# A branch prefetch hint at the head of the four long edge loops of a graph network on one core

## The reference

```python
def mesh_conv(x, src, dst, ea, w1, b1, g, bt, w2, b2):
    m = jnp.concatenate([x[dst], x[src], ea], axis=-1) @ w1 + b1
    m = jax.nn.silu(group_norm(m, g, bt))
    m = m @ w2 + b2
    out = jax.ops.segment_sum(m, dst, num_segments=n)
    return out / jnp.clip(cnt, 1.0)[:, None]
...
logits = (q[dst] * k[src]).sum(-1) * scale + (edge_attr @ ew + eb)
amax = jax.ops.segment_max(logits, dst, num_segments=n)
pe = jnp.exp(logits - amax[dst])
o = jax.ops.segment_sum(w[:, :, None] * v[src], dst, num_segments=n)
...
return h + o
```

## Time and profile before

| what | us |
|---|---|
| median of 3 runs | 8504.54 |
| lowest and highest | 8486.66, 8512.32 |
| span of the profiled execution | 11374.7 |
| first convolution, about | 343 to 3166 of the span |
| second convolution | 3519 to 6376 |
| logits | 6714 to 9799 |
| softmax | 9885 to 11248 |

### The profile page before, as it was taken

How to read it: one execution, slowest core, us unless ns; L and a number is a source line. 1 busy time by engine, 2 the same in 40 slices (tenths; PEclk the granted TensorE clock), 3 DMA queues, 4 the chain that set the end, 5 groups by cost and what they waited for, 6 DMA issues and landing times. The chain is left out here.

```text
span 11374.7 us, 252728 instructions
## 1 busy us (share of the span) xinstructions
PE 8397.2 (74%) x47420; PEld 6078.2 (53%) x47421; DVE 5534.1 (49%) x14001; ACT 4454.4 (39%) x7058; POOL 4607.9 (41%) x4729
## 2 busy tenths in 40 slices
PE   2777777777737777777777567777777777799885
PEld 2444444444434444444444456666665555688775
DVE  5444444444454444445444533333344445566555
ACT  3333333333323333333333233444444445555552
POOL 1555555545515555555555144444444444100000
PEclk8778878878867778788878755555555555555555
DMA  4333333333313333333333144444444444454442
GB/s 143 92 95 94 95 94 94 93 89 94 90 31 91 90 91 94 92 94 94 91 93 91 44 130 134 135 133 132 134 131 130 125 125 123 127 161 149 140 135 85
DMA packets 986405, 1222.46 MB, mean 107 GB/s; under 512 B 302171, under 2 KB 630054, under 8 KB 984874
## 3 DMA queue, kind: packets, MB, share of 16 engines
q1 hardware_dynamic: 760558, 707.74, 21.9%
q0 software_dynamic: 225792, 514.10, 17.2%
HBM read 1079.77 MB, written 141.49 MB: 107 GB/s over the span
## 5 line engine op out<-in xcount | busy, mean ns | idle before, releaser
L794 POOL DMA_INDIRECT conv_rows<-src_table,conv_idx x3136 | 3084.6, 984 | 2780.5 <-issue 1011.3
L1213 POOL DMA_INDIRECT lg_rows<-kv_table,lg_idx x1568 | 1482.1, 945 | 1816.9 <-issue 1042.4
L714 PEld LDWEIGHTS ps<-conv_vals,conv_hot 128*128 128x128 f32 x7024 | 1136.9, 233 | 991.9 <-DVE acc L700 540.3
L897 DVE TENSOR_REDUCE conv_var<-conv_sq 128x32 f32<-128x512 f32 x784 | 536.5, 684 | 2268.4 <-ACT conv_sq L858 1930.5
L714 PE MATMUL ps<-conv_vals,conv_hot 128*128 128x129 f32 x7024 | 1196.7, 323 | 416.3 <-DVE acc L700 316.5
L858 ACT ACTIVATE conv_sq<-ps 128x512 f32<-128x512 f32 x784 | 468.1, 597 | 2521.1 <-DMA hidden<-in_x_rows 1949.4
L839 PE MATMUL ps<-conv_y,ident 128*128 128x512 f32 x1568 | 1036.5, 747 | 318.3 <-DVE conv_y L927 295.3
L634 PE MATMUL ps<-dst_parts,conv_pick 128*128 x10536 | 946.5, 239 | 427.0 <-issue 411.2
L1271 ACT ACTIVATE acc<-ps,neg_win 128x512 f32<-128x512 f32 x976 | 627.1, 684 | 1253.1 <-issue 657.4
L714 PE MATMUL ps<-sm_vals,sm_hot 128*128 128x136 f32 x3512 | 956.2, 453 | 138.1 <-DVE acc L700 78.5
L634 PE MATMUL ps<-dst_parts,lg_pick 128*128 x5268 | 653.8, 304 | 541.2 <-ACT lg_pick L619 450.3
(11 more groups left out here) (209 smaller groups left out, 11359.0 us busy)
## 6 DMA issues: line engine op xcount, KB each, us to landing
conv_dst<-dst_rows SPq DMA_DIRECT2D x784, 256.0 KB
acc<-dst_rows SPq DMA_DIRECT2D x392, 256.0 KB
v_edges<-lg_rows SPq DMA_DIRECT2D x392, 256.0 KB
sm_dst<-dst_rows SPq DMA_DIRECT2D x392, 256.0 KB, 3.3
sm_v<-v_edges SPq DMA_DIRECT2D x392, 256.0 KB, 2.6
conv_rows<-src_table,conv_idx POOLq DMA_INDIRECT x3136
conv_ea<-ea_parts SPq DMA_DIRECT2D x784, 36.0 KB
lg_rows<-kv_table,lg_idx POOLq DMA_INDIRECT x1568
```

Source lines behind the costliest of these rows:

```text
L714: last = pe.matmul(bank(SUMS[g])[:, 0:self.width], self.hot[g][:, j, :], vals[:, j, 0:self.width], start=(j == 0), stop=(j == TILES - 1))
L794: pool.indirect_dma_start(rows[r][:, j, :], None, src_table, bass.IndirectOffsetOnAxis(idx[r][:, j:j + 1], 0)).then_inc(S["rows_in"][r], 16)
L1213: pool.indirect_dma_start(rows[r][:, j, :], None, kv_table, bass.IndirectOffsetOnAxis(idx[r][:, j:j + 1], 0)).then_inc(S["rows_in"][r], 16)
```

## The change

The flag changes nothing else: the inner loops (L569) and the loops over the nodes are as before. In the changed file 18 empty lines at the top are gone, so its line numbers are 18 lower (the loop is L86).

```diff
@@ slots @@
     tail = -(-last_lag // DEPTH)
     for i in range(tail + 1):
         turn(i)
-    with eng.Fori(tail + 1, ITERS) as i:
+    with eng.bass.Fori(tail + 1, ITERS, engines=(eng.engine,), hint_back_edge=True) as i:
         turn(i)
     for i in range(ITERS, ITERS + tail):
         turn(i)
```

## The result

The changed kernel takes 8539.01 us as the median of five runs (8530.18 to 8543.14), the kernel before 8504.54 us (8486.66 to 8515.55). The ratio is 1.0037, with a 95% interval of 1.0026 to 1.0047: 0.37% slower, some 32 us. That lies in the forecast's range (8450 to 8590) but not in its likeliest case: not within 0.3%, and four times the 8 us that the sum gave.

A forecast was written before the change was run, and what follows sets the result against it. It took PE to bound the softmax and a round trip of SP, POOL and PE the other passes. SP's 7 us and PE's 1 us, the rest hidden, gave + 8 us on 8504.5, 8512 us; range 8450 to 8590.

The forecast's parts named there:

- likeliest case: Whole kernel: a hint of 30 to 70 ns, mostly hidden; within 0.3% of before, 8490 to 8530 us, chance 0.55.
- second rival: Slow side: the hint makes the engine do something each turn, over 0.07 us on the path; 8593 us, chance 0.28.
- last sign: The forecast counts as wrong if the hint costs over 0.1 us on SP or PE.
- No code is fetched per turn: All loops: bodies stay with their engines; one packet per instruction queue in the first convolution, so 0 us saved.
- third rival: Code is fetched each turn now, PE's longest body paying; the hint saves 933 us, time about 7570, chance 0.04.
- rule of the Trainium skill: An engine keeps two pages of code; a taken branch outside them must fetch its page before execution goes on.
- The price of a hint: Each of 1819 hints, one per turn per engine, was taken at 50 ns, with 305 ns as the upper end.
- On PE the sequencer runs ahead where PE is behind, above all in the softmax, where PE is the bound: nothing there: PE's hints, above all in the softmax: hidden because the sequencer is ahead of a busy PE; no cost.
- the 1 us for PE: PE's hint on the round trip of loads where its queue is empty: 1 us.
- SP's hint on the round trip: Passes with an index load: the hint delays that load; 14.5 us if always on the path, about half taken, 7 us.
- The cover of DVE's and ACT's hints: Their hints disappear in waits: 828 us over 91 turns, 9 us a turn; uncovered, DVE's would cost 19 us.
- The first, a cheaper branch: The hint makes the closing branch cheaper, 0.17 us a turn; 49 us gained, 8455 us, up to 130 us, chance 0.13.

The follow-up runs named there:

- e8_hint_pe_softmax: Changed kernel with one hint in place of 19, at the head of PE's softmax loop; ratio 1.0031 to the kernel before.
- e9_hint_all_but_pe_softmax: Changed kernel with 18 hints, all but that of PE's softmax loop; ratio 0.9963 to the kernel before.
- e12_spare_bf16: Changed kernel without hints, PE's small signalling matmul using the bf16 identity in place of the fp32 one; ratio 1.0009 to the kernel before.
- e1_no_hint: Changed file with no hint at all, the zero of the series; 8499.94 us, ratio 0.9999 to the kernel before.
- e2_hint_late: Changed kernel with each of the 19 hints moved to the end of the body, ahead of the addition and closing branch; 8521.55 us, ratio 1.0027.
- e4_hint_dve_act: Changed kernel with hints on DVE and ACT alone, eight of the 19 loops; 8512.11 us, ratio 1.0014 to the kernel before.
- e3_move_head: Changed kernel with a plain register move in place of the hint at each long loop's head; 8506.57 us, ratio 1.0011.
- e10_moves_pe_softmax: Changed kernel without hints, four register moves meant for PE's softmax turn but absent from the trace; ratio 1.0004 to the kernel before.
- e11: Changed kernel without hints, one buffer for the softmax picks in place of two, so their address is constant; ratio 1.0021 to the kernel before.

## Why the prediction was right, and where it was wrong

The time lies in the range because the range was made wide enough for the second rival; the forecast's own 8490 to 8530 missed it, and its main step failed. By the last sign that the prediction gives it was wrong, too: a hint was to cost at most 0.1 us on SP or PE. Alone it takes 86 ns on SP and 99 ns on PE, but with all that it brings a turn of PE in the softmax is 0.31 us longer. That the time is inside is luck as far as the mechanism goes.

**No code is fetched per turn** (right). The queues have 20 and 34 packets in all, as in the earlier trace rows. With it fell the third rival, and the rule of the Trainium skill behind it (Runtime: NRT & Kernel Launch, Instruction fetch mechanics) had nothing to act on here: by the packets, no loop of this kernel outgrows what its engine keeps.

**The price of a hint** (right as far as it went). 31 to 44 ns in place of 50. What it occupies is more: from its start to the next instruction's on PE in the softmax 99 ns as a mean over 94 turns (9.3 us in all, by the starts in the trace), twice the 50 ns of the sum. On DVE and ACT it costs 52 and 45 ns more at each other branch while it stands. The prediction counted one instruction a turn and no effect on others, and had the price of a dear hint only as a rival.

**"On PE the sequencer runs ahead where PE is behind, above all in the softmax, where PE is the bound: nothing there"** (wrong, and this is the failed step; with it the 1 us for PE in the sum). I read 90% busy in the earlier trace rows as an array that is late, with a sequencer well ahead of it. In this pass the array is late because its sequencer is: for a super tile it does a register load, some twenty register operations and two or more branches, and the matmuls that begin a sum follow within 97 to 122 ns. e8_hint_pe_softmax shows the step alone: 27.8 us; e9_hint_all_but_pe_softmax shows that without it the pass loses nothing; e12_spare_bf16 shows that the array's work isn't what counts. The account from the two traces, over 94 turns of the pass, from each sequencer instruction's start to the next one's: the hint itself 9.3 us; 845 inner branches 8.4 us more, 10 ns each (those that fall through went from 67 to 70 ns, those that are taken from 209 to 222 ns, and there is more behind them than their own duration); the closing branch 1.3 us. That is 19 of 29.4 us. The other 10 us are spread, above all over L616, L543, L692, L533 and L584, whose instructions (but for those of L584) are no slower themselves but start later after one another; why, the traces don't say.

**SP's hint on the round trip, 7 us** (wrong in its ground). The round trip of the earlier trace rows was that of the profile at 11,374.7 us. In the convolution of e1_no_hint (1000 to 2200 us) POOL has one large row of waits left, and it is no wait:

```profile
POOL conv_rows L776 <- issue: 269.3, 884, 0.3
```

The waits for the index load, 348.3 us of 2700 in the earlier trace rows, are 10.7 us of 1200 here and 8.2 with the change. The gap of 0.3 us between gathers is nearly all the idle time POOL shows: POOL's gathers set the pace of the convolutions, its sequencer runs ahead of them as the prediction said, and all hints together moved the start of the softmax by 1.2 us in this pair of profiles (it is 2.1 us later in e2_hint_late and 6.0 in e4_hint_dve_act, so one pair tells no more than some us). The cover of DVE's and ACT's hints was judged rightly, and in the softmax it was deep enough even for branches that are twice as dear.

**The rivals.** The first, a cheaper branch, exists and is worth nothing here: from DVE's closing branch to its next instruction it is 203 ns in the first convolution in place of 335 and 285 in place of 335 in the second. The hint that now comes first takes 78 ns of that, so what came next before starts 54 ns earlier in the first and 25 ns later in the second, and DVE waits anyway. On PE the closing branch is no cheaper (216 to 234 ns). The second, a hint that costs more than 0.07 us a turn on the path, is what happened, with 0.28 of the chances; not by a fetch or a lookup, but by its slot and by the other branches. I had put the place of it on SP and PE in the passes with gathers.

**What stays open.** No run shows what a plain instruction in the hint's place would cost, since the moves of e3_move_head and e10_moves_pe_softmax didn't lengthen PE's turn. e2_hint_late cost 0.27% with its inner branches healed, of which its profile puts 12 us into the softmax and 2 us elsewhere, less than the 21 us between the medians. e4_hint_dve_act cost 0.14%, 12 us, without any in the softmax; in its profile the softmax begins 6.0 us later, and where the rest is I can't say. And the gain of e9_hint_all_but_pe_softmax at 11,300 us has no cause that I could show. Its profile is shorter than those of e8, e10 and e11, from the same session, in both convolutions: by 25 to 44 us in the first and by 47 to 58 in the second, and within 5 us in the logits. That execution, at 11273.43 us, was also the fastest of its twelve.

## What to carry to other kernels

Before a branch hint is set, count the instruction packets while the loop runs: with none, no fetching is there to be saved, and the hint isn't free. Its price is one slot a turn plus a rise of the other branches that the engine meets while the hint stands, so a long loop with short loops inside is the wrong place where that engine's sequencer sets the pace. And an engine that is busy for 90% of a pass needn't be the bound: take some work from the array and see whether the pass gets shorter; here 68 us less work gave 3 us, while 80 ns of sequencer time a turn came out whole. And a wait that a profile puts down to another engine can be one for the engine's own sequencer: look how long the engine named had been done.

## What the runs showed of the hardware

- A standing hint slows other compare branches of its engine: DVE 43 to 95 ns, ACT 34 to 79, PE 67 to 70 (taken ones 209 to 222), as medians. With the hint moved behind them they are at 43, 34 and 67.
- The same program took 8,500 us in some sessions and 11,280 to 11,360 in others. The runs at 8,500 us with a chip on record were on chip 15, the others on chips 1, 8 and 12, so a session and a chip can't be told apart here. In the slower ones, sequencer instructions that take some tens of ns stood for 700 ns and more now and then (the earlier trace rows has maxima of 727 and 852 ns on SP, the profile after 51 and 75). In the profile before, 446 register operations and branches of over 400 ns lie in the first convolution, 445 in the second, 1252 in the logits and none in the softmax. The convolutions and the logits are the longer ones there, while the softmax pass was the same to 1 us: 1398.4 us in e1_no_hint, 1398.5 in e10_moves_pe_softmax. That these stalls make the difference isn't shown, nor what causes them.
